# Reordered weight and input loads, and a split first key product, in a fused attention and expert kernel

## The reference

```python
x = x + xattn(layernorm(x), ctx, mask)      # x 8x64x512, ctx 8x1601x512, 16 heads of 32
x = x + attn(layernorm(x), W_q)             # (h W_q) h^T h for each sequence, no softmax
x = x + ffn(layernorm(x))                   # 8 experts, top 2

# xattn: q = h @ q_w.T + q_b ; k = ctx @ k_w.T + k_b ; v = ctx @ v_w.T + v_b
#        softmax(q k^T / sqrt(32), masked) v
# ffn:   logits = h @ gate_w + gate_b; top 2 of 8, softmax over the two
#        for e in range(8): out += cw[:, e] * (relu(h @ w1[e] + b1[e]) @ w2[e] + b2[e])
#        w1 8x512x2048, w2 8x2048x512
```

## Time and profile before

| | us |
|---|---|
| median of 3 runs | 1366.5 (1365.25 to 1367.12) |
| profiled execution | 1364.21 |
| its span, first to last instruction | 1362.4 |
| TensorE busy | 1286.7 (94%) |
| VectorE busy | 806.8 (59%) |
| ScalarE busy | 675.5 (50%) |
| GpSimd busy | 161.1 (12%) |
| chain that ended last, share on TensorE | 92% |

### The profile page before, as it was taken

One profiled execution on the slowest core, in us unless ns is written; L12 is line 12 of the kernel. 1 busy time (PEld: TensorE's weight loads), 2 busy tenths in 40 slices (PEclk: granted clock), 3 DMA queues, 4 the chain that ended last, 5 costly groups with the idle time before them and its releaser, 6 DMA issues.

```text
span 1362.4 us, 23006 instructions
## 1 busy us (share of the span) xinstructions
PE 1286.7 (94%) x9009; PEld 1201.0 (88%) x9009; DVE 806.8 (59%) x2052; ACT 675.5 (50%) x1192; POOL 161.1 (12%) x87
## 2 busy tenths in 40 slices
PE   6999999999999999999999999977559999999996
PEld 6699999999999999999999999976548999988995
DVE  5356656666666566565665666657326566565664
ACT  5345445535544645544554553453134566666661
POOL 3003002201300400400310120010300000000030
PEclk9999999999999999999999999997669999999998
DMA  8002200300300220220220030040135666666652
GB/s 289 10 1 86 75 1 27 134 1 2 131 30 1 86 75 1 86 75 1 82 79 1 26 119 1 1 165 1 62 136 199 235 230 203 212 235 231 213 181 64
DMA packets 61429, 129.07 MB, mean 95 GB/s; under 512 B 3492, under 2 KB 21040, under 8 KB 61080
## 3 DMA queue, kind: packets, MB, share of 16 engines
q1 hardware_dynamic: 59160, 120.85, 25.8%
q0 software_dynamic: 2176, 6.95, 1.6%
HBM read 121.89 MB, written 15.34 MB: 101 GB/s over the span
## 4 chain that ended last, share of the span: by engine, by line
PE 92%; DVE 3%; ACT 2%; DMA 1%; issue 1%; POOL 1%; SPq 0%; DVEq 0%
PE work L792 34%; PE ptp L792 23%; PE pv L895 7%; PE ptp L882 6%; PE work L830 6%; PE ptp L1062 2%; PE ptp L1063 2%; PE ptp L1064 2%; PE ptp L1066 2%; PE ptp L1065 2%; PE work L799 1%; PE ptp L799 1%; DVE pt L1239 1%; ACT pt L541 1%; POOL x_rows L522 1%
## 5 line engine op out<-in xcount | busy, mean ns | idle before, releaser
L792 PE MATMUL ptp<-vw_hi,cx_hi 128*128 128x256 f32 x832 | 241.7, 291 | 0.0
L792 PE MATMUL ptp<-vw_lo,cx_hi 128*128 128x256 f32 x832 | 235.2, 283 | 0.0
L792 PE MATMUL ptp<-vw_hi,cx_lo 128*128 128x256 f32 x832 | 235.0, 282 | 0.0
L481 POOL TENSOR_TENSOR cx_lo<-raw,cx_hi 128x1664 fp32r<-128x1664 f32 x31 | 117.6, 3793 | 676.5 <-ACT cx_hi L541 676.5
L792 PE MATMUL work<-cx_hi,kw_hi 128*128 128x402 f32 x512 | 179.2, 350 | 10.2 <-DVE cx_lo L1176 8.5
L792 PE MATMUL work<-cx_lo,kw_hi 128*128 128x402 f32 x512 | 178.6, 349 | 0.0
L792 PE MATMUL work<-cx_hi,kw_lo 128*128 128x402 f32 x512 | 177.6, 347 | 0.0
L792 PEld LDWEIGHTS ptp<-vw_hi,cx_hi 128*128 128x128 f32 x832 | 158.9, 191 | 16.9 <-issue 16.9
L792 PE MATMUL work<-xg_hi,w_hi 128*128 128x192 f32 x512 | 142.1, 278 | 23.6 <-DVE xg_lo L1391 23.6
L1239 DVE TENSOR_TENSOR pt<-ptp,pt 128x512 fp32r<-128x512 f32 (+1 forms) x224 | 141.3, 649 | 34.7 <-ACT pt L541 31.2
L792 PEld LDWEIGHTS ptp<-vw_lo,cx_hi 128*128 128x128 f32 x832 | 159.1, 191 | 0.0
(11 more groups left out here) (217 smaller groups left out, 2495.1 us busy)
## 6 DMA issues: line engine op xcount, KB each, us to landing
w1raw<-in_w SPq DMA_DIRECT2D x32, 1024.0 KB, 5.2
w2raw<-in_w SPq DMA_DIRECT2D x32, 1024.0 KB, 6.0
raw<-in_ctxT SPq DMA_DIRECT2D x32, 832.0 KB, 5.8
pr<-in_mask SPq DMA_DIRECT2D x8, 800.5 KB, 4.4
xrow<-x_rows SPq DMA_DIRECT2D x7, 256.0 KB, 2.7
y_rows<-y_out_rows POOLq DMA_DIRECT2D x7, 256.0 KB, 2.4
kwraw<-in_kwT SPq DMA_DIRECT2D x2, 512.0 KB, 4.9
xin<-in_x SPq DMA_DIRECT2D x1, 1024.0 KB, 9.5
```

The lines of the kernel that those rows point to most:

```text
L481: pool.tensor_tensor(cx[1][:, :, sl], raw[:, k % 2], cx[0][:, :, sl].bitcast(F32), ALU.subtract).then_inc(c_lo, 1)
L792: last = pe.matmul(dst, lhs(i, c), rhs(j, c), start=(c == 0 and (i, j) == (0, 0)), stop=(c == n - 1 and (i, j) == (1, 0)))
```

## The change

It has two parts.

The 24 products of key blocks 6 and 7, with their wait for the low part of chunk 3, have moved from ahead of the queries to between them and the scores. The core of the diff:

```diff
@@ -375,17 +379,21 @@
                 cols = slice(h * D // 2, (h + 1) * D // 2)
                 sp.dma_start(kwraw[:, :, cols], kwT[:, cols].rearrange("(c p) n -> p c n", p=P)).then_inc(ld_kw[h], 16)
 
-            load_kw(0)
-            load_chunk(0, 0, True)
+            for cs, kw_sem, c_sem in ((FIRST_C, ld_kw0, ld_c0), (REST_C, ld_kw[0], ld_raw[0])):
+                rows = slice(cs.start * P, cs.stop * P)
+                sp.dma_start(kwraw[:, cs, 0:D // 2], kwT[rows, 0:D // 2].rearrange("(c p) n -> p c n", p=P)
+                             ).then_inc(kw_sem, 16)
+                sp.dma_start(raw[:, 0, cs], ctxT[0:1, rows, 0:CC].rearrange("o (c p) n -> p (o c) n", p=P)
+                             ).then_inc(c_sem, 16)
             load_chunk(0, 1, True)
             sp.dma_start(xin[:], x.rearrange("(t p) d -> p t d", p=P)).then_inc(ld_x, 16)
+            sp.dma_start(qwraw[:], qwT.rearrange("(c p) n -> p c n", p=P)).then_inc(ld_qw, 16)
             load_chunk(0, 2)
-            load_kw(1)
-            sp.dma_start(qwraw[:], qwT.rearrange("(c p) n -> p c n", p=P)).then_inc(ld_qw, 16)
             load_chunk(0, 3)
             for a in range(2):
                 sp.dma_start(vwraw[:, a], vwT[a * D // 2:(a + 1) * D // 2, :].rearrange("(b p) n -> p b n", p=P)
                              ).then_inc(ld_vw, 16)
+            load_kw(1)
             load_mask(0)
 
             def first_rows(e):
@@ -436,15 +444,15 @@
 
             def expert(ph, e, fresh=False, last=False):
                 for p in range(NP):
-                    if p == 1 and not last:
-                        if fresh:
-                            sp.wait_ge(x_sent, 16 * 2 * TT)
-                        load_x(ph, e + 1)
                     if p < NP - 1:
                         load_w1(ph, e, p + 1, fresh and p == 0)
                     elif not last:
                         load_w1(ph, e + 1, 0)
                     load_w2(ph, e, p, fresh and p < 2)
+                    if p == 1 and not last:
+                        if fresh:
+                            sp.wait_ge(x_sent, 16 * 2 * TT)
+                        load_x(ph, e + 1)
 
             def experts(ph):
                 load_w1(ph, 0, 0, ph == 0)
@@ -481,8 +489,8 @@
                 pool.tensor_tensor(cx[1][:, :, sl], raw[:, k % 2], cx[0][:, :, sl].bitcast(F32),
                                    ALU.subtract).then_inc(c_lo, 1)
 
-            pool.wait_ge(c_lo, 1)
-            for k in range(1, NKC):
+            pool.wait_ge(c_lo, 2)
+            for k in range(2, NKC):
                 ctx_lo(0, k)
             for b in range(1, B):
                 for k in range(NKC):
@@ -573,33 +581,40 @@
                     act.wait_ge(w_full, j + 1)
                     key_hi(0, j, j % 4)
 
+            act.wait_ge(consts, 2)
+            act.activation(stat[:, 60:61], ones[:, 0:1], ACT.Sqrt)
             act.wait_ge(t_full, 1)
             copy(biasT[:], pv[:, 0:3 * C], t_out)
-            def kw_hi(h):
-                cols = slice(h * D // 2, (h + 1) * D // 2)
-                act.wait_ge(ld_kw[h], 16)
-                copy(kw[0][:, :, cols], kwraw[:, :, cols], w_hi)
-
-            kw_hi(0)
-            ctx_hi(0, 0)
+            first = slice(0, D // 2)
+            act.wait_ge(ld_kw0, 16)
+            copy(kw[0][:, FIRST_C, first], kwraw[:, FIRST_C, first], kw0_hi)
+            act.wait_ge(ld_c0, 16)
+            copy(cx[0][:, FIRST_C, 0:CC], raw[:, 0, FIRST_C], c0_hi)
+            act.wait_ge(ld_kw[0], 16)
+            copy(kw[0][:, REST_C, first], kwraw[:, REST_C, first], w_hi)
+            act.wait_ge(ld_raw[0], 16)
+            copy(cx[0][:, REST_C, 0:CC], raw[:, 0, REST_C], c_hi)
             ctx_hi(0, 1)
             act.wait_ge(t_out, 1)
-            first_keys(range(0, 1))
+            first_keys(range(0, 2))
             root(1, range(TT))
-            first_keys(range(1, 2))
             ctx_hi(0, 2)
             first_keys(range(2, 4))
             for c in range(C):
                 act.wait_ge(t_full, c + 2)
                 copy(xnT[:, c], yb[c][:], t_out)
+            first_keys(range(4, 5))
             ctx_hi(0, 3)
-            kw_hi(1)
+            first_keys(range(5, 6))
             act.wait_ge(ld_vw, 32)
             copy(vw[0][:].rearrange("p (a b) n -> p a b n", a=2), vwraw, w_hi)
-            first_keys(range(4, FIRST_K))
             for c in range(C):
                 act.wait_ge(t_full, C + 2 + c)
                 act.activation(qT[:, c], yb[c][:], ACT.Identity, bias=biasT[:, c:c + 1]).then_inc(q_done, 1)
+                if c == 1:
+                    act.wait_ge(ld_kw[1], 16)
+                    copy(kw[0][:, :, D // 2:D], kwraw[:, :, D // 2:D], w_hi)
+            first_keys(range(6, FIRST_K))
 
             def exponentials(b, r):
                 act.wait_ge(nmx_done, 8 * b + r + 1)
@@ -849,8 +864,17 @@
                 elif kind == "v":
                     value_item(a, k, bank)
 
-            pe.wait_ge(w_lo, 1)
-            for j in range(4):
+            READY = {(0, 0): ((kw0_hi, w_hi), (c0_hi, c_hi)), (0, 1): ((c0_lo, c_lo),), (1, 0): ((kw0_lo, w_lo),)}
+            for m in range(2):
+                for i, j in PASSES:
+                    for c in range(C):
+                        if m == 0 and c % (C // 2) == 0:
+                            for ready in READY[i, j]:
+                                pe.wait_ge(ready[c // (C // 2)], 1)
+                        last = pe.matmul(work[m][:, 0:KC], kw[i][:, c, m * P:(m + 1) * P], cx[j][:, c, 0:KC],
+                                         start=(c == 0 and (i, j) == PASSES[0]), stop=(c == C - 1 and (i, j) == PASSES[-1]))
+                last.then_inc(w_full, 1)
+            for j in range(2, 4):
                 key_item(0, 0, j, work[j])
             pe.wait_ge(ln1, TT)
             pe.wait_ge(t_out, 1)
@@ -858,7 +882,7 @@
                 for t in range(TT):
                     last = pe.transpose(yb[c][:, t * P:(t + 1) * P], xin[:, t, c * P:(c + 1) * P], ident[:])
                 last.then_inc(t_full, 1)
-            for j in range(4, FIRST_K):
+            for j in range(4, 6):
                 pe.wait_ge(w_free, j - 3)
                 key_item(0, 0, j, work[j % 4])
             pe.wait_ge(t_out, C + 1)
@@ -866,6 +890,9 @@
             for m_ in range(C):
                 plain(yb[m_][:], lambda c: qwraw[:, c, m_ * P:(m_ + 1) * P],
                       lambda c: xnT[:, c]).then_inc(t_full, 1)
+            for j in range(6, FIRST_K):
+                pe.wait_ge(w_free, j - 3)
+                key_item(0, 0, j, work[j % 4])
             pe.wait_ge(w_lo, 3)
             pe.sem_inc(pt_used, PTD)
 
@@ -1166,14 +1193,18 @@
                 dve.wait_ge(w_hi, i)
                 dve.tensor_tensor(w[1], whole, w[0].bitcast(F32), ALU.subtract).then_inc(w_lo, 1)
 
-            def kw_lo(h):
-                cols = slice(h * D // 2, (h + 1) * D // 2)
-                weight_lo(h + 1, [w[:, :, cols] for w in kw], kwraw[:, :, cols])
-
             step(dve.memset(negmask[:, LK:LKP], LOWEST))
-            kw_lo(0)
-            dve.wait_ge(c_hi, 1)
-            dve.tensor_tensor(cx[1][:, :, 0:CC], raw[:, 0], cx[0][:, :, 0:CC].bitcast(F32),
+            first = slice(0, D // 2)
+            for cs, kw_ready, kw_done, c_ready, c_done in ((FIRST_C, kw0_hi, kw0_lo, c0_hi, c0_lo),
+                                                           (REST_C, w_hi, w_lo, c_hi, c_lo)):
+                dve.wait_ge(kw_ready, 1)
+                dve.tensor_tensor(kw[1][:, cs, first], kwraw[:, cs, first], kw[0][:, cs, first].bitcast(F32),
+                                  ALU.subtract).then_inc(kw_done, 1)
+                dve.wait_ge(c_ready, 1)
+                dve.tensor_tensor(cx[1][:, cs, 0:CC], raw[:, 0, cs], cx[0][:, cs, 0:CC].bitcast(F32),
+                                  ALU.subtract).then_inc(c_done, 1)
+            dve.wait_ge(c_hi, 2)
+            dve.tensor_tensor(cx[1][:, :, CC:2 * CC], raw[:, 1], cx[0][:, :, CC:2 * CC].bitcast(F32),
                               ALU.subtract).then_inc(c_lo, 1)
             dve.wait_ge(ld_x, 16)
             layer_norm(xin, xin, ln1, 1)
@@ -1273,15 +1304,16 @@
                     convert_mask(b + 1)
 
             for j in range(FIRST_K):
-                if j == 4:
-                    kw_lo(1)
-                    weight_lo(3, [w[:].rearrange("p (a b) n -> p a b n", a=2) for w in vw], vwraw)
+                if j == 6:
+                    weight_lo(2, [w[:].rearrange("p (a b) n -> p a b n", a=2) for w in vw], vwraw)
+                    dve.wait_ge(consts, 5)
+                    dve.wait_ge(q_done, 2)
+                    query_blocks(0, 0)
+                    weight_lo(3, [w[:, :, D // 2:D] for w in kw], kwraw[:, :, D // 2:D])
                     convert_mask(0)
                 dve.wait_ge(kv_hi, j + 1)
                 key_lo(0, j, j % 4)
             dve.wait_ge(q_done, C)
-            dve.wait_ge(consts, 5)
-            query_blocks(0, 0)
```

(4 more changed lines are left out.)

## The result

The changed kernel takes 1333.1 us (median of 4 runs, 1332.8 to 1335.7), the kernel before 1365.9 beside it (4 runs, 1364.1 to 1367.1). The ratio is 0.9763, 95% interval 0.9748 to 0.9779: 32.8 us less. The forecast was 1334.5, with a range of 1331 to 1341.

What follows compares the result with a forecast made beforehand. TensorE is busy nearly everywhere, so only the start and the entry to the experts can give time. 22.5 + 3.3 + 6.2 = 32.0 us off the profiled 1364.2 gives 1332.2; plus 2.3 for the median, 1334.5, range 1331 to 1341.

Steps and rivals of the forecast that it cites:

- Term 1: Entry to the experts: with both loads early, TensorE restarts at 981.1 instead of 1003.58, 22.5 us less.
- Term 2: First 48 expert products: they run at the 2.4 GHz level, 5.34 us instead of 8.65, 3.3 us less.
- The rival with the low clock: After the gather the clock stays low, the 3.3 us gain is gone: 1337.8 us, chance 0.07.
- The wait before 30.96: Start: TensorE stood 1.9 us, then 24 products ran at the high level at once; argument that a short gap keeps the clock.
- What is late next: Expert entry: w1 piece 3 and w2 piece 2 still stand behind the written rows, landing by 997.6; cost 0.
- the slack of 10 us: Expert entry: w1 piece 3 is wanted after products ending near 1015 and needs 1.9 + 2.3 conversion; over 10 us spare.
- the slower rival: Expert loop: expert rows queued behind the loads land too late, each of seven turns waits; 1366 to 1370 us, chance 0.01.
- Term 3: Start, up to the first score: 46.15 instead of 52.36, 6.2 us less.
- the landing of chunk 2: Start: chunk 2 lands at 17.3 by bytes at 379 KB/us, so keys 4 and 5 start at 22.9.
- the bank wait: Start: the second pair of scores waits for the bank where key 7 lay; 0.7 us added, with hand-overs.
- the prediction's own signs: Wrong if a new TensorE wait stands between 985 and 1020, or normalising steps are untouched and keys 4, 5 after 24.
- The port conflict: Start: GpSimd's chunk 2 step holds VectorE's fourth normalising step, keys 4 and 5 2.3 us later: 1336.8 us, chance 0.30.

Runs made afterwards that it cites:

- The split of the expert part by load: Two runs on the kernel before, one expert 0 load each ahead of the wait for written rows: w2 piece 1 1343.7 us, w1 piece 2 1361.4 us.
- start alone: The kernel before with only the start part of the change, experts in their old order: 1359.9 us, ratio 0.9965.
- w1 piece 2 alone early: The kernel before with only w1 piece 2 of expert 0 issued ahead of the wait for the written rows: 1361.4 us.

## Why the prediction held, point by point

**Term 1**, the restart, 22.5 us: measured 22.4. Its steps stood: the pieces go out near 940 (935.3 and 935.7), ScalarE and VectorE have w2 piece 1 converted before the gather ends (w1 piece 2 follows later, unneeded till then), and what remains is 1.26 us of high and low part (forecast 1.1). The split of the expert part by load shows that the reading of the chain was right in its object, w2 piece 1.

**Term 2**, the clock, 3.3: measured 3.2. After a gap of 1.26 us the granted clock was 1.00 over the 48 products. The rival with the low clock is out here; but the lower level did come 12 us later, with the eight bias products, which I had not looked at. There the bias stretch got shorter by 1.5 us than in the profile of before and the block behind it longer by 1.5, so between these two it cost nothing. (The wait before 30.96, from which I argued, was 1.71 us in its row and not 1.9; the argument is the same.)

**What is late next**: nothing for TensorE. w1 piece 3 and w2 piece 2 were issued at 985.80 and 986.44, ScalarE waited 2.85 us, and the slack of 10 us took it. The expert loop keeps its 41.5 us per expert; TensorE never waited for the expert rows issued behind the loads, so the slower rival is out.

**Term 3**, the start, 6.2: this is the mis-sized one, it gave 4.4. The step that failed is the landing of chunk 2. I had it at 17.3 by bytes at 379 KB/us; it was at 18.75. With whole loads it is at 17.26 and 17.29, so the rate was right for whole loads and wrong for the four half loads, which nothing in the trace of before showed; the windows account for 0.6 of the difference and the rest is open. The rest of the walk is close: first key product 6.61 (forecast 6.7), blocks 0 to 3 done at 19.6 (19.7), keys 4 and 5 at 24.40 (22.9), the queries 13.74 (13.75), the bank wait 0.61 (0.7). The 1.5 us late in keys 4 and 5 and 0.2 in their products make nearly all of the 1.8 missing. By the prediction's own signs this part was wrong: it named four untouched normalising steps with keys 4 and 5 after 24 as such a sign, and that is what came, 1.92 us and 24.40. The first score stood at 47.11, outside its 45.5 to 46.2. What failed is the size of the term, by 1.8 of 6.2; chunk 2 was the gate, as it said. The norms began at 18.55 instead of 17.7, since chunk 1 was 0.9 late as well; that cost nothing by itself.

**The port conflict** was real and cost what was said of it where it struck the normalising steps: keys 4 and 5 at 26.37 and 26.78, 2.0 and 2.4 behind the changed kernel (forecast 2.3). Its chance of 0.30 rested on 0.1 us between two estimated times. In the first profile the fourth step moved by 0.9 us (to 19.99) and GpSimd by 1.5 (to 20.53), and all four profiles of this start missed the conflict, two of them by 0.15 us or less. That I called this rival the less likely was right by luck as much as by reading. The start of before falls to either side too (first value product at 53.66 and 53.48 without the conflict, at 55.16 and 55.66 with it, in four profiles of the same code), so the price of the conflict was already in some of its runs.

**The sum**: 32.0 forecast, 32.8 between the medians, 28.6 between the profiled spans. The sum was made from profile rows, and row for row it is 2.0 too high (30.0) and span for span 3.4. The forecast for the median then added 2.3, the distance of before's median from its profiled run; in after the median lies 2.6 below the profiled run. The two errors, 3.5 too low and 4.9 too high, largely cancel, so it is partly luck that 1334.5 came within 1.4 us of 1333.1. The attention stage between the marks varied from 917.9 to 920.8 us between runs of kernels that share it, which is as much as the gap between my sum and either number.

## What to carry to other kernels

In a hand-ordered queue look for what stands behind a long wait and needs nothing from it: here one load of 1 MB, queued behind a wait for written rows, kept an engine three hand-overs away idle for 23.65 us, and brought the clock down for the work behind. Before splitting a first transfer to start the big engine sooner, follow the chain to the next thing it will wait for; here it waited for chunk 2, and with that chunk's low part on VectorE whole loads were as good. And when two engines' steps come to lie within a microsecond of each other, take the conflict row from the trace and move one of the two, rather than count on the margin.

## What the runs showed of the hardware

- A GpSimd elementwise step of 3.7 to 4.0 us that reads SBUF holds a normalising step, or a VectorE step with two SBUF inputs, that begins within it to its very end, however small it is: 0.16 us became 3.60, and four steps of 1.92 together became 5.33 to 5.40. The statistics steps of the layer norm were not held: 2.47 us with and without.
- Loads of 256 and 416 KB in place of 512 and 832 KB: 305, 275 and 356 GB/s in three successive microseconds against 387, 391 and 386. In three of the eight profiles with the split loads the second key half was converted from 8.3 to 8.6 instead of 7.0 to 7.4, so the half loads also land less evenly.
- The second of GpSimd's indexed writes took 1.66 us in all eleven profiles in which VectorE makes the low part of w2 piece 1 beside it, and 0.97 in the three in which it does not (before, start alone, w1 piece 2 alone early). It cost TensorE nothing here. Rows of after and of before:

```profile
972.88 1.66 POOL L530 DMA_INDIRECT x_rows<-hn,row_i  x1 [0.30 <-issue]
```

```profile
977.28 0.97 POOL L522 DMA_INDIRECT x_rows<-hn,row_i  x1 [0.30 <-issue]
```

- The last 16 products of the kernel took 4.24 us in one profile, at a granted clock of 1.00, and 5.5 to 5.7 in the other 13, at means of 0.69 to 0.70 where I read them, with the same work ahead of them. What decides it stays open.
